# Expert layer: token numbers by one-hot products, rows gathered per tile, part of its weights and statistics made in the layer ahead

## The chip, the cores and the metric

The kernel runs on one core of one Trainium2 chip. The metric is the device time of one launch in microseconds, the median of three runs. A second number, the profiled execution, is one launch under the hardware profiler; all durations below are from it.

## What is computed

`x` is 4096 tokens by 256 numbers (128 sequences of 32 tokens). Six layers are added to it in turn, each on a layer norm of `x`. The three that the change touches:

```python
# first layer (x0): softmax attention of 32 queries over 257 keys, 16 heads of 16
scores = jnp.einsum('bhqd,bhkd->bhqk', q, k) / np.sqrt(D_K)
scores = jnp.where(mask[:, None, :, :] > 0, NEG, scores)
p = jax.nn.softmax(scores, axis=-1)
x = jnp.einsum('bhqk,bhkd->bhqd', p, v)
...
# fifth layer (a1): softmax self-attention over 32 tokens, 16 heads of 16
attn = jnp.einsum('bhid,bhjd->bhij', q, k) * scale + phi_bias(L)[None, None]
out = jnp.einsum('bhij,bhjd->bhid', jax.nn.softmax(attn, axis=-1), v)
...
# sixth layer (e1): each token goes to one of 8 experts (256 -> 1024 -> 256)
route_prob = jax.nn.softmax(t @ switch_w + switch_b, axis=-1)
routes = jnp.argmax(route_prob, axis=-1)
for e in range(n_experts):
    h = jax.nn.gelu(t @ w1[e] + b1[e])
    out = jnp.where((routes == e)[:, None], h @ w2[e] + b2[e], out)
out = out * jnp.max(route_prob, axis=-1)[:, None]
```

## The kernel before

`x` stays in SBUF as `all_xres`, 128 partitions by 32 tiles of 256. Products that need float32 accuracy are three float16 products of a high and a low part: ScalarE (ACT) rounds to the high part (`hi_...`), VectorE (DVE) or GpSimd (POOL) subtracts it from the source for the low part (`lo_...`). Each layer is one block in which the five engines run their own instruction streams and wait for one another by counting semaphores; the order on an engine is that of the code, written out by hand as one loop body with its stages taken from different steps. Layers are separated: the next block begins when all engines have left the one before.

**x0, softmax_attention.** A loop over 128 sequences. For each, TensorE (PE) makes keys and values, scores in two row groups of 64 rows (`scores`), eight transposes of the probabilities by the identity (`transposes`, L556, each 128 by 128 in float32), and products with the values in column groups of 32 (`attend`). PSUM tile `psT` of 1024 columns holds the transposes; ACT copies it in two pieces (`hi_pT`, L670) and DVE makes the low part in two (`lo_pT`, L804). PE's order in one sequence is keys, transposes, (an x tile's transposes), values, attend, scores.

**a1, self_attention.** 32 steps, each for one x tile (four sequences). The DVE order in a step: `add_max` of the next step (L2485, L2490), `lo_pT` (L2502), the residual of the step before (L2527, "all_xres"), `lo_xn` or `lo_k` of a later pair (L2463), `sum_recip` (L2495, L2497), in some steps `ln` (L176), `extract` (L2511, three times), `lo_ob` (L2518), `lo_q` or `lo_v` of a later pair. POOL spreads queries over heads (`a_qbdh`, `a_qbdl`, L2193), subtracts maxima (L2202), scales by the reciprocal sums (L2208) and adds the bias (L2216).

**e1, sort_tokens ("e1r").** Loads nine constants through SP's queue, makes the statistics of all tiles (`Statistics`, L149, then L152 to L164), and runs over the 32 tiles: normalise on DVE (L176), transpose on PE (L2660), copy on ACT (L2693), logits on PE (L2667). Between tiles, pieces of the expert weights (16 of 128x2048, loaded into two `stage` tiles) are split by ACT (`hi_w`, L2687) and DVE (`lo_w`, L2741): half of them here, half in the later part. Then the routing: softmax, the first best expert as a one-hot (`oh`), counts over tiles by two products with `tri` and `ones` (`psR`), two scans, and for every token its place in a list of 39 slots of 128 rows, each slot holding tokens of one expert. Every place of the list in HBM (`e_rows`, 5 MB) is filled with a pad row first (L2823), and POOL then scatters 32 tiles of rows (x, probability, token number, mean, reciprocal deviation) into it by indirect DMA (L2831), from row buffers that ACT fills with x (L2708) and DVE with the other numbers (L2809, L2811).

**e1, expert_tiles ("e1t").** 39 slots. SP loads a slot's rows from `e_rows` (L2890). DVE normalises (L3043), PE transposes (L2905) and makes the hidden products in two halves (`psH`, L2921 and L2922), ACT takes the low half sums out (`take_low`, L2971), DVE adds the bias (`add_bias`, L3059, four per half), ACT makes gelu (L2979) and its high part (`hi_hid`, L2987), POOL the low part (`lo_hid`, L3015), PE the second products (`psY`, L2933), DVE the result (L3067 to L3074), and POOL scatters it to the output (L3023).

## Time and profile before

| | before |
|---|---|
| median of 3 runs | 2874.72 us (2873.59 to 2875.07) |
| profiled execution, its own time | 2873.39 us |
| its span, first to last instruction | 2871.6 us |
| mean granted TensorE clock over the span | 0.933 of full |
| PE busy | 2442.8 us, 85% |
| VectorE (DVE) busy | 2156.5 us, 75% |
| ScalarE (ACT) busy | 1948.5 us, 68% |
| GpSimd (POOL) busy | 1579.3 us, 55% |

The busy time of an engine is the sum of its instructions; PE's ends are modelled and overlap, so 85% is an average over stages that are limited by different things. In the profile's picture of the span in 40 slices, x0 lies in the first third, a1 from about 2160 us on, e1r from 2444 us, e1t from 2586 us to the end. The TensorE clock is given as a share of 2.4 GHz: 1.00 is that, 0.50 is 1.2 GHz.

### The profile page before, as it was taken

What the parts mean: (1) busy time and instruction counts of PE and PEld (TensorE: products, weight loads), DVE (VectorE), ACT (ScalarE), POOL (GpSimd) and SP (SyncE); (2) the same over time, 40 slices, a digit from 0 to 9 for tenths busy, and PEclk for the clock granted to TensorE, in tenths of its full rate; (3) what the DMA queues carried; (4) which work ended last, traced back from release to release, by engine and by line L of the source; (5) the groups of instructions that cost most, each with busy time, mean ns of one, the idle gap of its engine ahead of it and who ended that gap; (6) DMA issues with size and microseconds to landing.
All of it is one profiled execution on the core that took longest, in us unless ns stands there. A gap on an engine that the chain in (4) does not pass through costs nothing. (4 is left out here: it accounts for less than half of the span.)

```text
span 2871.6 us, 96041 instructions
## 1 busy us (share of the span) xinstructions
PE 2442.8 (85%) x37734; PEld 1929.7 (67%) x37734; DVE 2156.5 (75%) x4991; ACT 1948.5 (68%) x4323; POOL 1579.3 (55%) x1680
## 2 busy tenths in 40 slices
PE   3999999999946999994969999999957887508997
PEld 2788888888834777762548888888846666506665
DVE  4899999999965999984447677777757887645665
ACT  2788888888847999962437777777736665335554
POOL 3777777777723555531027666766626776053444
PEclk9999999999976999997979999999978999559999
DMA  5222222222100000000022122212100000641110
GB/s 156 63 73 73 71 70 70 70 70 70 48 16 1 1 1 1 1 1 31 1 70 69 55 66 69 69 54 68 52 18 2 2 2 2 222 162 42 42 39 27
DMA packets 120676, 145.06 MB, mean 51 GB/s; under 512 B 12912, under 2 KB 111632, under 8 KB 118064
## 3 DMA queue, kind: packets, MB, share of 16 engines
q1 hardware_dynamic: 115568, 124.40, 14.5%
q0 software_dynamic: 4672, 14.57, 1.4%
q8 instruction: 308, 5.05, 0.7%
q14 instruction: 128, 1.05, 0.1%
HBM read 123.71 MB, written 15.22 MB: 48 GB/s over the span
## 5 line engine op out<-in xcount | busy, mean ns | idle before, releaser
L2068 DVE TENSOR_TENSOR_SCAN m_s<-m_a,m_psBx 128x2048 f32<-128x2048 f32 x64 | 282.7, 4417 | 21.6 <-PE m_psBx L1843 18.8
L1364 DVE SCALAR_TENSOR_TENSOR x_pTl<-x_psS,x_pTh 128x1024 f16<-128x1024 f32 x128 | 156.7, 1225 | 173.8 <-ACT x_pTh L1272 173.8
L662 ACT ACTIVATE x_prob<-x_prob,x_low 128x257 f32<-128x257 f32 x512 | 253.5, 503 | 9.8 <-DVE x_low L789 9.6
L1854 PE MATMUL m_psS<-m_s,all_ident 128*128 128x256 f32 x1024 | 238.4, 386 | 0.9 <-DVE m_s L2068 0.9
L1854 PEld LDWEIGHTS m_psS<-m_s,all_ident 128*128 128x128 f32 x1024 | 190.7, 191 | 43.3 <-issue 18.2
L789 DVE CUSTOM_DVE_ANT_0 x_prob<-x_psS,x_masked,x_prob 128x256 f32<-128x256 f32 x512 | 216.0, 477 | 1.1 <-PE x_psS L546 0.9
L1975 ACT ACTIVATE m_a<-m_dt,m_rate 128x248 f32<-128x248 f32 x512 | 205.8, 489 | 5.0 <-DVE m_s L2068 4.6
L678 ACT ACTIVATE x_kh<-x_psK,x_bk 128x256 f16<-128x256 f32 x256 | 107.5, 470 | 118.1 <-PE x_psK L430 118.1
L3015 POOL TENSOR_TENSOR e1t_hidl<-e1t_g,e1t_hidh 128x512 f16<-128x512 f32 x78 | 92.8, 1189 | 144.3 <-ACT e1t_hidh L2987 144.3
L804 DVE SCALAR_TENSOR_TENSOR x_pTl<-x_psT,x_pTh 128x512 f16<-128x512 f32 x256 | 163.2, 677 | 0.9 <-PE x_psO L572 0.9
L1053 POOL TENSOR_TENSOR x_qbdh<-x_qh,all_mask4h 128x1024 f16<-128x1024 f16 x32 | 60.6, 1895 | 181.1 <-DVE x_ql L1345 181.1
L1045 POOL TENSOR_TENSOR x_ctxl<-x_ctx,x_ctxh 128x512 f16<-128x512 f32 x128 | 149.6, 1168 | 10.7
L1285 ACT ACTIVATE x_vh<-x_psV 128x512 f16<-128x512 f32 x128 | 76.4, 597 | 115.9 <-PE x_psV L1092 115.9
L335 POOL TENSOR_TENSOR x_ctxl<-x_ctx,x_ctxh 128x512 f16<-128x512 f32 x128 | 149.0, 1164 | 10.7
L430 PE MATMUL x_psK<-x_ctxh,x_wkh 128*128 128x256 f16 x512 | 141.6, 277 | 5.7 <-POOL x_ctxl L335 5.0
L1266 ACT ACTIVATE x_psS<-x_psS 128x1024 f32<-128x1024 f32 x128 | 129.0, 1008 | 24.3 <-PE x_psS L1186 24.3
L1092 PE MATMUL x_psK<-x_ctxh,x_wkh 128*128 128x256 f16 x512 | 141.6, 277 | 3.3 <-POOL x_ctxl L1045 3.0
L670 ACT ACTIVATE x_pTh<-x_psT 128x512 f16<-128x512 f32 x256 | 138.9, 594 | 6.3 <-PE x_psT L556 2.1
L3059 DVE SCALAR_TENSOR_TENSOR all_xres<-e1t_psH,e1t_bias,all_xres 128x128 f32<-128x128 f32 x312 | 87.5, 343 | 72.8 <-ACT all_xres L2971 72.8
L1092 PE MATMUL x_psV<-x_wvh,x_ctxh 128*128 128x256 f16 x512 | 141.0, 275 | 0.6 <-issue 0.6
L1092 PE MATMUL x_psK<-x_ctxh,x_wkl 128*128 128x256 f16 x512 | 140.7, 275 | 0.0
L430 PE MATMUL x_psK<-x_ctxh,x_wkl 128*128 128x256 f16 x512 | 140.7, 275 | 0.0
(554 smaller groups left out, 10247.5 us busy)
## 6 DMA issues: line engine op xcount, KB each, us to landing
x_ctx<-in_ctxT SPq DMA_DIRECT2D x64, 1024.0 KB, 6.2
x_mraw<-in_mask SPq DMA_DIRECT2D x128, 128.5 KB, 2.8
e1r_stage<-in_L_ffn_w SPq DMA_DIRECT2D x16, 1024.0 KB, 5.1
e_rows<-e1r_pad POOLq DMA_DIRECT2D x1, 5070.0 KB, 19.5
e1t_row<-e_rows SPq DMA_DIRECT2D x39, 130.0 KB, 2.1
all_xres<-in_x SPq DMA_DIRECT2D x1, 4096.0 KB, 14.5
x_vxr<-x_vx SPq DMA_DIRECT2D x128, 32.0 KB, 3.6
x_vxr<-x_vx SPq DMA_DIRECT2D x96, 8.0 KB, 2.3
```

Source lines behind the costliest of these rows:

```text
L335: pool.tensor_tensor(lo[:, j], src, hi[:, j], ALU.subtract).then_inc(ctx_split, 1)
L430: last = pe.matmul(out, a, b, start=m == 0, stop=m == len(prods) - 1)
L662: act.activation(prob[c % 4][:, h, :], prob[c % 4][:, h, :], ACT.Exp, bias=low[c % 4][:, h:h + 1], scale=-1.0, accum_out=sm[c % 2][:, h:h ...
L670: act.activation(pT[c % 2][0][:, kt, :], psT[:, kt * 512:(kt + 1) * 512], ACT.Copy, scale=PS)\
L789: dve.tensor_tensor_reduce(prob[c % 4][:, h, 0:LAST], psS[:, to:to + LAST], masked[gp][:, j, 0:LAST], -SC, prob[c % 4][:, h, LAST:S2], ALU ...
L804: dve.scalar_tensor_tensor(pT[c % 2][1][:, kt, :], psT[:, kt * 512:(kt + 1) * 512], PS, pT[c % 2][0][:, kt, :], ALU.mult, ALU.subtract).th ...
L1045: pool.tensor_tensor(lo[:, j], src, hi[:, j], ALU.subtract).then_inc(ctx_split, 1)
L1092: last = pe.matmul(out, a, b, start=m == 0, stop=m == len(prods) - 1)
L1364: dve.scalar_tensor_tensor(pT[c % 4][1][:].rearrange("p r k n -> p (r k n)"), psS[c % 2][:], PS, pT[c % 4][0][:].rearrange("p r k n -> p ( ...
L1854: last = pe.matmul(psS[:, h * ST:(h + 1) * ST], con["ident"][:], S[h][:, :, m, :], start=m == 0, stop=m == NS - 1)
L1975: last = act.activation(A[h][:, :, m, 1:T], dt[c % 2][:, h, :].rearrange("p (b t) -> p b t", t=T)[:, :, 1:T], ACT.Exp, scale=rate[:, h, m: ...
L2068: dve.tensor_tensor_scan(rows(S), rows(A), psBx[:], 0.0, ALU.mult, ALU.add).then_inc(scan_done, 1)
```

## The change

Four parts.

1. **x0.** A transpose of 128 rows becomes two of 64 rows (one for each row group), with a 64x64 piece of the identity as the moving operand: 16 matmuls for 8. The results of a row group lie in one bank, and `hi_pT` and `lo_pT` take a bank each time (the same 2 x 128x512).
2. **a1.** Each of the 32 steps also splits a quarter of an expert weight piece (ACT `hi_w` and DVE `lo_w`, 128x512) and makes the `bn_stats` of the x tile finished in the step before (`count`). SP loads ten constants and eight 1 MB pieces, and writes each finished x tile to HBM (`x_dram`). Some of a1's tiles (`qp`, `K`, `vp`, `V`, `qbd`, `pT`) now lie in the part of the weight tile `ea_w` that is filled later; a1 and e1 share one scope ("ea").
3. **sort_tokens.** No statistics loop and no constant loads. Normalising alternates between DVE and POOL with four buffers. Four pieces of the weights are split in the tile loop, the last four after it: ACT scales the stage tile in place and rounds it (`scale_w`, two 128x2048 each), POOL subtracts (128x2048). The token list is made by matmuls: one-hot of the place in a tile (`oh_in`, 128 per token tile) times one-hot of the slot, with the tile number and with the row number as value (`named`), summed over 32 tiles in `psI` (128x78); from it the token number of each place (`token`). The pad fill, the row buffers and the 32 scatters are gone; only 4 numbers a token are written to `x_dram`.
4. **expert_tiles.** The rows of a slot are gathered from `x_dram` by indirect DMA on POOL's queue, three slots ahead, instead of loaded by SP. ACT's and DVE's orders within a slot are new.

```diff
 (x0, TensorE)
                 for kt in range(2):
                     for h in range(4):
-                        last = pe.transpose(psT[:, kt * 512 + h * P:kt * 512 + (h + 1) * P],
-                                            prob[c % 4][:, h, kt * P:(kt + 1) * P], con["ident"][:])
+                        for r in range(RG):
+                            rows, to = slice(64 * r, 64 * r + 64), r * 512 + (kt * 4 + h) * 64
+                            last = pe.transpose(psT[:, to:to + 64], prob[c % 4][rows, h, kt * P:(kt + 1) * P],
+                                                con["ident"][rows, rows])
...
 (x0, ScalarE; VectorE's lo_pT likewise)
-                for kt in range(2):
-                    act.activation(pT[c % 2][0][:, kt, :], psT[:, kt * 512:(kt + 1) * 512], ACT.Copy, scale=PS)\
-                        .then_inc(pt_hi, 1)
+                for r in range(RG):
+                    act.activation(turned(pT[c % 2][0], r), strip_of(psT, r), ACT.Copy, scale=PS).then_inc(pt_hi, 1)
...
 (a1, SyncE)
+            for g in range(NT):
+                if g % 4 == 0:
+                    wait(sync, w_lo, g)
+                    sync.dma_start(stage[:], d["L1_ffn_w"][g // 4]).then_inc(w_in, 16)
+                if g:
+                    keep_rows(sync, g - 1)
...
 (a1, ScalarE and VectorE)
+            def hi_w(i, c):
+                g = i * 2 * U + c
+                act.wait_ge(w_in, (g // 4 + 1) * 16)
+                act.activation(ahead.W[:, g // 4, 0, quarter(g)], stage[:, quarter(g)], ACT.Copy, scale=WS).then_inc(w_hi, 1)
...
+            def lo_w(i, c):
+                g = i * 2 * U + c
+                dve.wait_ge(w_hi, g + 1)
+                dve.scalar_tensor_tensor(ahead.W[:, g // 4, 1, quarter(g)], stage[:, quarter(g)], WS,
+                                         ahead.W[:, g // 4, 0, quarter(g)], ALU.mult, ALU.subtract).then_inc(w_lo, 1)
+
+            def count(i, c):
+                g = i * 2 * U + (c - 1)
+                dve.wait_ge(x_done, g + 1)
+                dve.bn_stats(ahead.stats[:, g * 6:(g + 1) * 6], xres[:, g * D:(g + 1) * D]).then_inc(ahead.counted, 1)
...
 (sort_tokens, ScalarE behind its tile loop)
+            act.wait_ge(meta_ready, 4)
+            act.dma_start(x_dram[0:TOK, D:ROW].rearrange("(t p) k -> p t k", p=P), meta[:]).then_inc(meta_out, 16)
+            scale_w(LATE - BY_POOL)
+            act.wait_ge(tile_ready, 1)
+            act.activation(named[:, :, 1, :], oh_tile, ACT.Copy, scale=row[:]).then_inc(row_ready, 1)
+            for k in range(LATE - BY_POOL + 1, LATE):
+                scale_w(k)
...
 (sort_tokens, GpSimd)
+            for k in range(LATE - BY_POOL, LATE):
+                hi, lo = halves(k)
+                pool.wait_ge(w_hi, k + 1)
+                pool.tensor_tensor(lo, stage[k % 2][:], hi, ALU.subtract).then_inc(w_lo_pool, 1)
...
 (sort_tokens, VectorE)
+            did(dve.tensor_tensor(oh_tile, slot[:].unsqueeze(1).to_broadcast([P, NT, SLOTS]),
+                                  at_hi[:].unsqueeze(2).to_broadcast([P, NT, SLOTS]), ALU.is_equal))
+            did(dve.tensor_tensor(named[:, :, 0, :], oh_tile, tile[:].unsqueeze(2).to_broadcast([P, NT, SLOTS]), ALU.mult))
+            dve.sem_inc(tile_ready, 1)
...
-                pool.indirect_dma_start(rows_dram, bass.IndirectOffsetOnAxis(ap=idx[c][:], axis=0), row[c][:],
-                                        None).then_inc(placed[c], 16)
...
 (expert_tiles, ScalarE)
                     if exists(i, c, 0):
-                        take_low(i, c, 0)
                         if exists(i, c, 1):
                             hi_xn(*at(i, c, 1))
+                        take_low(i, c, 0)
+                        take_low(i, c, 1)
                         gelu(i, c, 0)
                         hi_hid(i, c, 0)
-                        take_low(i, c, 1)
                         gelu(i, c, 1)
...
 (expert_tiles, GpSimd)
+            def gather(i, c):
+                s = i * U + c
+                wait(pool, o_done, s - U + 1)
+                pool.indirect_dma_start(row[c][:], None, x_dram, bass.IndirectOffsetOnAxis(ap=token[:, s:s + 1], axis=0))\
+                    .then_inc(row_in[c], 16)
...
 (expert_tiles, VectorE)
-                    if exists(i, c, 2):
-                        normalise(*at(i, c, 2))
                     if exists(i, c, 1):
                         lo_xn(*at(i, c, 1))
                     if exists(i, c, 0):
                         add_bias(i, c, 0)
                         add_bias(i, c, 1)
+                    if exists(i, c, 2):
+                        normalise(*at(i, c, 2))
```

On VectorE in the self-attention, from `lo_ob` of one step to `lo_pT` of the next, before:

```order
L2518 SCALAR_TENSOR_TENSOR a_obl<-a_o,a_obh 128x256
L2463 TENSOR_TENSOR a_ql<-a_psQK,a_qh 128x512
L2485 SCALAR_TENSOR_TENSOR a_prob<-a_psS,all_phi 128x256 x2
L2490 TENSOR_REDUCE a_mx<-a_prob 128x16
L2502 SCALAR_TENSOR_TENSOR a_pTl<-a_psT,a_pTh 128x512
```

and with the change (`ea_w` is the weight tile, and also the name of the tiles that a1 has lent from it):

```order
L2566 SCALAR_TENSOR_TENSOR a_obl<-a_o,a_obh 128x256
L2511 TENSOR_TENSOR ea_w<-a_psQK,ea_w 128x512
L2578 BN_STATS ea_stats<-all_xres 128x6
L2572 SCALAR_TENSOR_TENSOR ea_w<-a_stage,ea_w 128x512
L2533 SCALAR_TENSOR_TENSOR a_prob<-a_psS,all_phi 128x256 x2
L2538 TENSOR_REDUCE a_mx<-a_prob 128x16
L2550 SCALAR_TENSOR_TENSOR ea_w<-a_psT,ea_w 128x512
```

Two instructions are put in ahead of the next step's `add_max`.

On ScalarE in the sort phase, from the last tile of the loop to the end of the block, before:

```order
L2693 ACTIVATE e1r_row<-e1r_psX 128x256 x4
L2702 ACTIVATE e1r_ex<-e1r_lg 128x256
L2687 ACTIVATE e_w<-e1r_stage 128x2048
L2708 ACTIVATE e1r_row<-all_xres 128x256 x4
L2687 ACTIVATE e_w<-e1r_stage 128x2048
L2708 ACTIVATE e1r_row<-all_xres 128x256
L2708 ACTIVATE e1r_xn<-all_xres 128x256 x2
L2708 ACTIVATE e1r_pad<-all_xres 128x256
```

and with the change:

```order
L2772 ACTIVATE e1r_xnT<-e1r_psX 128x256 x2
L2776 ACTIVATE e1r_ex<-e1r_lg 128x256
L2778 DMA e_x<-e1r_meta 128x32x4
L2764 ACTIVATE e1r_stage<-e1r_stage 128x2048
L2767 ACTIVATE ea_w<-e1r_stage 128x2048
L2781 ACTIVATE all_xres<-all_xres,ea_row 128x32x39
L2764 ACTIVATE e1r_stage<-e1r_stage 128x2048
L2767 ACTIVATE ea_w<-e1r_stage 128x2048
L2764 ACTIVATE e1r_stage<-e1r_stage 128x2048
L2767 ACTIVATE ea_w<-e1r_stage 128x2048
L2764 ACTIVATE e1r_stage<-e1r_stage 128x2048
L2767 ACTIVATE ea_w<-e1r_stage 128x2048
L2671 UNCONDITIONAL_BRANCH
```

The copies of x into row buffers (L2708) are gone; the second `scale_w` stands behind the activation that waits for VectorE's one-hot of the slots (L2781).

On ScalarE in one slot of the expert tiles, before:

```order
L2965 ACTIVATE e1t_bias<-e_b 128x8
L2971 ACTIVATE all_xres<-e1t_psH 128x512
L2958 ACTIVATE e1t_xnp<-e1t_psX 128x256
L2979 ACTIVATE e1t_g<-all_xres 128x512
L2987 ACTIVATE e1t_hidh<-e1t_g 128x512
L2971 ACTIVATE all_xres<-e1t_psH 128x512
L2979 ACTIVATE e1t_g<-all_xres 128x512
L2987 ACTIVATE e1t_hidh<-e1t_g 128x512
```

and with the change:

```order
L3010 ACTIVATE e1t_bias<-ea_b 128x8
L3003 ACTIVATE e1t_xnp<-e1t_psX 128x256
L3016 ACTIVATE all_xres<-e1t_psH 128x512 x2
L3024 ACTIVATE e1t_g<-all_xres 128x512
L3032 ACTIVATE e1t_hidh<-e1t_g 128x512
L3024 ACTIVATE e1t_g<-all_xres 128x512
L3032 ACTIVATE e1t_hidh<-e1t_g 128x512
```

Both copies of the low sums (L2971, now L3016) stand together ahead of the first gelu, and the high part of the next slot's x ahead of them.

## Rows read from the trace of the kernel before

**Rows 1.** Windows: busy (count) of PE, PEld, DVE, ACT, POOL; clock, DMA share, GB/s.

```profile
100.00:760.00 660.00, 648.77 (x12743) 545.62 (x12741) 634.38 (x1993) 554.43 (x1711) 471.28 (x700) 1.00 0.25 71
2160.00:2420.00 260.00, 209.84 (x3686) 174.24 (x3686) 216.68 (x412) 169.04 (x301) 192.56 (x147) 0.97 0.01 2
2470.00:2513.00 43.00, 40.26 (x191) 37.10 (x191) 30.23 (x43) 23.54 (x39) 0.00 (x0) 0.50 0.56 190
2620.00:2850.00 230.00, 212.57 (x1684) 151.37 (x1684) 140.91 (x437) 134.61 (x271) 113.97 (x102) 1.00 0.13 38
```

**Rows 2.** Timeline of PE and its loads in one sequence of x0: start, us, count.

```profile
302.66 0.27 PE L430 MATMUL x_psV<-x_wvh,x_ctxl 128*128 128x256 f16 x1
302.86 0.21 PE L572 MATMUL x_psO<-x_pTh,x_vh 128*32 128x64 f16 x4
...
305.43 1.04 PE L556 MATMUL x_psT<-all_ident,x_prob 128*128 128x128 f32 x8
306.31 0.38 PE L450 MATMUL x_psM<-all_ident,x_xn 128*128 128x128 f32 x2
```

**Rows 3.** Timeline of PE at the end of the sort's tile loop.

```profile
2511.83 1.71 PE L2667 MATMUL e1r_psL<-e1r_sw,e1r_row 128*128 128x8 f32 x8
```

**Rows 4.** Timeline of a1, VectorE and GpSimd, at the end of a step.

```profile
2317.07 0.74 DVE L2485 SCALAR_TENSOR_TENSOR a_prob<-a_psS,all_phi 128x256 f32<-128x256 f32 x2
2317.23 1.90 POOL L2193 TENSOR_TENSOR a_qbdh<-a_qh,all_mask4h 128x1024 f16<-128x1024 f16 x1 [2.58 <-DVE a_ql L2463]
```

**Rows 5.** Line L2518 of VectorE: duration ns min/median/max over its 32 instructions.

```profile
L2518 DVE SCALAR_TENSOR_TENSOR a_obl<-a_o,a_obh x32: 425/426/1103, 2178.1 to 2441.8; 128x256 f16<-128x256 f32 x32
```

**Rows 6.** Timeline, three engines, from a1's last residual to the end of the routing.

```profile
2443.83 0.42 DVE L2527 SCALAR_TENSOR_TENSOR all_xres<-a_psY,all_xres 128x256 f32<-128x256 f32 x1 [1.55 <-PE a_psY L2248]
2452.67 0.28 DVE L2720 MEMSET e1r_pad<- 128x260 f32 x1 [8.42 <-DMA e1r_tokid<-in_rt_tokid]
2453.76 10.55 DVE L149 BATCH_NORM_STATS2 e1r_ln_stats<-all_xres  x32
2470.32 0.73 DVE L176 TENSOR_SCALAR e1r_xn<-all_xres,all_mean,all_rstd 128x256 f32<-128x256 f32 x2
2472.33 2.28 DVE L2741 SCALAR_TENSOR_TENSOR e_w<-e1r_stage,e_w 128x2048 f16<-128x2048 f32 x1
2513.58 0.42 DVE L2762 TENSOR_TENSOR e1r_lg<-e1r_psL,e1r_s_bias 128x256 f32<-128x256 f32 x1 [1.81 <-PE e1r_psL L2667]
2515.28 1.89 ACT L2687 ACTIVATE e_w<-e1r_stage 128x2048 f16<-128x2048 f32 x1
2521.94 0.69 DVE L2780 TENSOR_TENSOR_SCAN e1r_inc<-e1r_go_on,e1r_tot 128x256 f32<-128x256 f32 x1
2526.10 0.42 DVE L2795 TENSOR_REDUCE e1r_m<-e1r_lg 128x32 f32<-128x256 f32 x1
```

**Rows 7.** Timeline from the last scatter to the first expert product.

```profile
2579.45 0.96 POOL L2831 DMA_INDIRECT e_rows<-e1r_pad,e1r_idx  x1 [0.30 <-issue]
2585.52 3.65 SPq L2890 DMA_DIRECT2D e1t_row<-e_rows  x8
2587.66 0.87 DVE L3043 TENSOR_SCALAR e1t_xn<-e1t_row 128x256 f32<-128x256 f32 x2 [14.41 <-DMA e1t_row<-e_rows]
```

**Rows 8.** Lines of GpSimd, whole kernel, and the page's DMA issues.

```profile
L122 POOL TENSOR_TENSOR f_w1l<-f0w_stage,f_w1h 128x2048 f16<-128x2048 f32 x1 | 4.1, 4061 | 9.5 <-ACTq L97 9.5
...
e1r_stage<-in_L_ffn_w SPq DMA_DIRECT2D x16, 1024.0 KB, 5.1
```

**Rows 9.** Waits from 2620 to 2850 us: us in total, times, longest.

```profile
ACT e1t_g L2979 <- DVE all_xres L3059: 91.9, 67, 1.8
...
PEld e1t_psY L2933 <- issue: 21.7, 34, 0.8
PE e1t_psY L2933 <- POOL e1t_hidl L3015: 17.2, 34, 0.6
```

**Rows 10.** Timeline of VectorE, expert tiles: the bias additions of one half.

```profile
2689.92 1.12 DVE L3059 SCALAR_TENSOR_TENSOR all_xres<-e1t_psH,e1t_bias,all_xres 128x128 f32<-128x128 f32 x4
```

More of the change, by code:

```diff
@@ L2583, in sort_tokens @@
-def sort_tokens(nc, d, xres, con, norm, W, b1, b2, owner, rows_dram):
-    E, SLOTS, PIECE = 8, owner.shape[1], 2048
-    ID, ROW = D + 1, D + 4
-    NPIECE = 2 * E
-    U, ROUNDS = 8, NPIECE // 4
+        b2 = sp.sb("b2", [P, E * D], F32)
+        owner, token = sp.sb("owner", [P, SLOTS], I32), sp.sb("token", [P, SLOTS], U32)
+        sort_tokens(nc, d, xres, con, norm, ahead, b2, owner, token)
+        expert_tiles(nc, xres, con, ahead, b2, owner, token, out)
+def sort_tokens(nc, d, xres, con, norm, ahead, b2, owner, token):
+    E, SLOTS, ROW = 8, owner.shape[1], D + 4
+    LATE, BY_POOL = 16 - AHEAD, 4
+    W, x_dram, consts = ahead.W, ahead.x_dram, ahead.consts
+    sw, s_bias, tri, ones, desc, slot, place_in, tile, row = (consts[k] for k in (
+        "sw", "s_bias", "tri", "ones", "desc", "slot", "place_in", "tile", "row"))
@@ L2743, in body, with lo_w @@
-            def body(i):
-                for c in range(U):
-                    ln(i, c)
-                    if c % 4 == 3:
-                        lo_w(i, c // 4)
-            run(dve, body)
+            dve.wait_ge(ahead.counted, NT)
+            statistics.finish(dve, norm)
+            dve.sem_inc(stats_ready, 1)
+            def lo_w(k):
+                hi, lo = halves(k)
+                dve.wait_ge(w_hi, k + 1)
+                dve.scalar_tensor_tensor(lo, stage[k % 2][:], WS, hi, ALU.mult, ALU.subtract).then_inc(w_lo, 1)
```

375 lines of the change are left out of this document (192 added, 183 removed).

## The prediction

> **What bounds the kernel now.** I read the windows first, stage by stage [rows 1]. In x0 (100 to 760 us) PE is busy 648.8 of 660 us and VectorE 634.4: both are nearly full, so either can become the bound. The clock is 1.00. In a1 (2160 to 2420) no engine is: PE 209.8, VectorE 216.7 and GpSimd 192.6 of 260 us, a cycle of waits. A step takes 8.6 us. In the sort's tile loop (2470 to 2513) PE is busy 40.3 of 43 us at a clock of 0.50, so PE sets the pace at 1.2 GHz. In the expert tiles (2620 to 2850) PE is busy 212.6 of 230 us; 34 slots in 230 us make 6.76 us each. The waits there tell what the rest is: PE waits for the low part of the hidden values 17.2 us in 34 slots, its weight loads stand 21.7 us ahead of the same products, and ScalarE waits 91.9 us for VectorE's bias additions [rows 9]. That is ScalarE and VectorE taking turns inside a slot, half by half, each half costing VectorE 1.12 us [rows 10].
>
> The timeline around the sort shows the largest stretch without PE work. From a1's last residual at 2443.8 to the first normalised row of the expert tiles at 2587.7 it is 143.8 us [rows 6, 7], and in it nothing overlaps with the layers on either side.
>
> **x0, transposes in halves.** Eight transposes take 0.88 us from the first to what follows, 0.11 each [rows 2]. What limits them? The logit products of the sort have a moving operand of 8 columns and still take 0.214 us each at half clock (1.71 us for 8) [rows 3], so loading 128 float32 columns costs 0.107 us at full clock, which is the same 0.11. The change has 16 loads of 128 columns. If the two row groups load side by side, as it has to be for them to be worth it, they take 0.88 again; if one behind the other, 16 x 0.107 = 1.71, 0.85 more for each of 128 sequences. No row shows float32 loads of two row groups. I take side by side. What is certain is that PE now changes the shape of its array around the transposes. From the last product of the values (0.11 apart within the run) to the first of the column groups is 0.20 us [rows 2], 0.09 more than inside a run. Two more such changes in a sequence are 0.18 us, 23 us in 128 if all of it shows. PE idles 1.7% and VectorE 4% of the time [rows 1], so part is absorbed: I take **+14 us**, between 0 and 23 if loads go side by side, and up to +110 (128 x 0.85) if not. The copies of ScalarE and VectorE keep their count and size.
>
> The Trainium skill (TensorEngine Tiling (Array Packing), Key Properties) says that changing the tiling mode drains TensorE, and the 0.09 us agree. The same page (Theoretical Speedup) gives up to 2x for operands of at most 64 rows; estimated by it, the eight pairs would take half, 56 us less of PE in x0. The row of the 8-column products speaks against that, because there the load has the time and not the moving side.
>
> **a1, two more VectorE instructions a step.** In the cycle, `add_max` of the next step follows `lo_q` without a pause [rows 4], and everything behind it (`lo_pT`, PE's attend, `extract`) waits for it. So what is put ahead of it adds in full. `count`: 10.55 us for 32 bn_stats is 0.33 [rows 6]. `lo_w` at 128x512: a quarter of 2.28 is 0.57 [rows 6], I take 0.60. Together 32 x 0.93 = 29.8 us. Then the neighbour: `a_obl` (two inputs in SBUF) takes 0.43 us as a rule but up to 1.10 [rows 5], when GpSimd works at the same time. `lo_w` also has two inputs in SBUF, and in the step that ends with `lo_q` GpSimd begins its spread of 1.90 us 0.16 us after `add_max` would begin [rows 4]; `lo_w` begins 0.33 after that point and would stand until GpSimd is done, some 1.55 us. This meets 14 of the even steps; of it 0.47 comes back, since the next spread then no longer meets `a_obl`. 14 x (1.55 - 0.47) = 15. Sum **+44 us**, from +30 (no block) to +52 (blocked also by other spreads). ScalarE's 0.6 us a step for `hi_w` lies in its 35% of idle time [rows 1], and the DMAs (8 MB loaded, 4 MB written over 275 us, at a DMA share of 0.01 now) cost nothing.
>
> The Trainium skill (SBUF — State Buffer, Who interferes with whom) states this as an exclusive lock of a port pair between GpSimd and a VectorE instruction with two SBUF inputs, held for a whole instruction. By it the block is full and not a slowdown, which is the 1.10 against 0.43 in the row; a share of bandwidth would have made it a few tenths.
>
> **Sort, until the end of its tile loop.** Now 2443.83 to 2513.58, 69.8 us [rows 6]. Away: the wait for the constants behind a1 (to 2452.67, of it 0.75 for the change of block stays), 7.7; filling pad and go_on, 1.1; bn_stats 10.55; four of eight `hi_w` in the loop, each of which puts ScalarE's copies off. The loop takes 43.26 us for 32 tiles, and 32 x 1.17 (PE's eight products at half clock) is 37.4; the rest, 5.9 us over eight pieces, is 0.55 a piece after the first ones' start, so 2.2 back. New: one `count` 0.33, and `lo_w` of the last piece near the end, 1. Sum **-20 us**, the loop ending 49.5 us after the last residual. I keep the clock at 0.50, because PE is busy 94% of the window at that clock and does not leave it [rows 1].
>
> **Sort, behind the loop.** Let R be the end of the loop. Before, the first row of the expert tiles is normalised at R + 74.1 (2513.6 to 2587.7) [rows 6, 7]: routing 14.7, 32 scatters and their landing, then a change of block and a load of 2.1. With the change there are two chains. VectorE's: the scan stands at R + 8.4 now, and GpSimd's first late piece (a 128x2048 subtraction is 4.06 [rows 8], started when ScalarE's two passes of 1.89 [rows 6] are over, R + 8.1) holds it till R + 12.2, 3.8 later; the places are then known at R + 16.8, the slot one-hot and its product with the tile number (1248 columns each, about 1.4) at R + 20.5. The weights': ScalarE stands at that one-hot and begins piece 5 at R + 21.8; two passes 3.8, GpSimd 4.1 until R + 29.7; only then is the stage tile free for piece 7, whose load is 5.1 [rows 8], R + 34.9; two passes, 38.7; GpSimd 4.1, R + 42.8. The token numbers (32 products of 78 columns, five short VectorE steps) are there near R + 31, so the weights end it. Change of block 2.6 (the 5.1 us from the last scatter to the first load [rows 7], less its landing), gather 1.0 to issue and 2.4 to land: R + 49. **-25 us**. Both parts of the sort: **-45**, from -36 to -53.
>
> **Expert tiles.** The low sums of both halves are taken together, so VectorE adds the bias of the second half while ScalarE is at the first gelu. ScalarE's 134.6 us / 34 = 3.96 a slot plus one wait of 1.12 - 0.58 makes 4.5 us, VectorE's 140.9 / 34 = 4.1 [rows 1, 10]: both below PE. PE's wait of 17.2 / 34 = 0.51 goes, at most the 0.64 of its loads [rows 9]. The larger, times 38 slots, is **-25 us**; -10 if GpSimd's two more instructions a slot (a gather of about 1 us, as the scatter) hold its low parts back.
>
> **Sum.** +14 +44 -45 -25 = -12 us against the profiled execution's 2873.39, 2861; the median of the runs shown is 1.3 above that execution, so **2862 us**.
>
> **Rivals.**
> 1. *As summed*, within the bounds of its terms (2845 to 2880). Chance 0.50. Three quarters of it is more than 0.2% below 2874.7 (5.7 us, what a measurement of this kernel can tell from none).
> 2. *The halved transposes really run in half the time.* Then VectorE at 96% is what is left, worth 20 us at most in x0; with +14 gone the sum is about 2833. For it: score products of two row groups already run side by side. Against: the 8-column row. 0.10.
> 3. *Loads of the row groups go one behind the other.* +110 in place of +14: 2958, slower. For it: nothing shows a pair of float32 loads. 0.08.
> 4. *Slower through a1 alone*: `lo_w` meets a GpSimd instruction in every step, not in 14. GpSimd is busy 74% of the time there [rows 1]. Then 32 x (0.93 + 1.55) = 79, in place of 44: 2897. It decides from +62 on. Against: in odd steps the place behind `lo_v` has no spread beside it. 0.14.
> 5. *The clock rises* in the sort's loop, because PE now idles 7 us and not 27 ahead of it. The loop is then paced by ScalarE and the pieces, some 17 us shorter: 2845. 0.10.
> 6. *The expert order does nothing*: the slots keep 6.76 us, another alternation takes the place. 2887, slower. 0.08.
>
> Faster: 0.37 of case 1, with 0.10 and 0.10 of cases 2 and 5, 0.57. Slower: 0.08, 0.14 and 0.08 of cases 3, 4 and 6, and 0.01 of case 1, 0.31. Same: the rest of case 1, 0.12. The range from 2838 to 2898 holds cases 1, 4, 5 and 6 and leaves out 2 and 3, 0.18.
>
> **What would show it.** In x0: 5.5 to 5.7 us a sequence, transposes 0.9 us in total with an 0.2 us gap on both sides; if 1.7, rival 3. In a1: a two-step of 19.9 us in place of 17.2, with a `lo_w` of about 2.1 us in every second step and 0.6 in the others. In the sort: a tile loop at 0.50 that takes 41 us, ScalarE waiting for the one-hot of the slots, and a last GpSimd subtraction ending the block near R + 43. In the expert tiles: a slot of 6.13 us without a PE wait for `e1t_hidl`. Wrong by most would be the x0 term, which is multiplied by 128 and has no row of its own.

## The result, and the profile after

| | before | changed |
|---|---|---|
| median | 2874.89 us (2873.59 to 2875.56, 4 runs) | 2898.78 us (2897.48 to 2901.02, 4 runs) |
| span of the profiled execution | 2871.6 us | 2899.2 us |
| ratio | | 1.0081, 95% interval 1.0068 to 1.0094 |

The change makes the kernel 24 us slower, where 12 us faster was forecast; 2898.78 lies just above the end of the forecast range, 2898. Read at the same landmarks in both traces, the 27.6 us between the spans come from these stages:

| stage, from and to | before | changed | difference | forecast |
|---|---|---|---|---|
| x0: until the last transpose of probabilities starts | 812.3 | 802.8 | -9.5 | +14 |
| from there until a1's first maximum | 1352.0 | 1352.6 | +0.6 | 0 |
| a1: first maximum to last residual | 279.5 | 338.2 | +58.7 | +44 |
| sort: last residual to the end of its tile loop | 69.8 | 53.5 | -16.3 | -20 |
| sort: end of the loop to the first normalised slot | 74.1 | 47.6 | -26.5 | -25 |
| expert tiles: first normalised slot to last result | 276.2 | 293.2 | +17.0 | -25 |
| last result to the end | 7.7 | 11.3 | +3.6 | 0 |

Windows of the changed kernel (PE, PEld, DVE, ACT, POOL busy, clock, DMA share), which answer to [rows 1]:

```profile
100.00:750.00 650.00, 632.32 (x13621) 503.95 (x13620) 633.62 (x1989) 539.89 (x1709) 470.62 (x702) 1.00 0.25 72
2190.00:2420.00 230.00, 172.96 (x2704) 146.38 (x2702) 190.74 (x347) 129.42 (x236) 142.89 (x109) 0.90 0.12 42
2502.00:2545.00 43.00, 37.95 (x185) 35.66 (x184) 12.68 (x19) 18.41 (x36) 25.40 (x16) 0.50 0.29 100
2640.00:2870.00 230.00, 227.45 (x1565) 149.79 (x1563) 141.40 (x408) 128.63 (x253) 135.36 (x125) 1.00 0.12 37
```

In the expert tiles PE is now busy 227.5 of 230 us, almost without a wait, and yet does fewer products than before (x1565 for x1684 in the same 230 us). In a1 the clock has fallen from 1.00 in that stretch to 0.90.

**x0.** Timeline of PE; it answers to [rows 2]:

```profile
309.06 0.27 PE L442 MATMUL x_psK<-x_ctxh,x_wkl 128*128 128x256 f16 x1
309.26 0.71 PE L570 MATMUL x_psT<-all_ident,x_prob 64*128 64x64 f32 x16
309.90 0.31 PE L482 MATMUL x_psM<-all_ident,x_px 128*96 128x128 f32 x1
```

The 16 transposes take 0.64 us to what follows, where 8 took 0.88. The start times of the single records show how: the two transposes of a pair, one in each row group, start 0.003 us apart, and from the second pair on one pair follows the other after 0.061 us, where whole transposes followed after 0.109. The 0.64 us also hold a first pair of 0.11 us and 0.15 us from the last pair to the product behind, with its other shape. With the shape change ahead (0.20 after the last key product, 0.11 inside a run) about 0.15 us less a sequence are left; 0.07 of it arrives (9.5 / 128). That VectorE, now busy 633.6 of 650 us, takes up the rest is likely and not shown by a run.

**a1.** The line of `lo_w` (duration ns min/median/max), and the timeline of VectorE and GpSimd at the end of an even step; they answer to [rows 5] and [rows 4]:

```profile
L2572 DVE SCALAR_TENSOR_TENSOR ea_w<-a_stage,ea_w x32: 666/676/2271, 2171.0 to 2492.3; 128x512 f16<-128x512 f32 x32
```

```profile
2444.33 0.42 DVE L2578 BATCH_NORM_STATS2 ea_stats<-all_xres 128x6 f32<-128x256 f32 x1
2444.50 1.89 POOL L2235 TENSOR_TENSOR ea_w<-ea_w,all_mask4h 128x1024 f16<-128x1024 f16 x1 [2.08 <-DVE ea_w L2511]
2444.67 2.27 DVE L2572 SCALAR_TENSOR_TENSOR ea_w<-a_stage,ea_w 128x512 f16<-128x512 f32 x1
2446.86 0.74 DVE L2533 SCALAR_TENSOR_TENSOR a_prob<-a_psS,all_phi 128x256 f32<-128x256 f32 x2
```

The block is where it was foreseen: 13 of the 32 `lo_w` take 2.27 us (14 were forecast), the one shown until 0.55 us after the end of GpSimd's spread at 2446.39; the others take 0.67. A block as whole as this is what the Trainium skill (SBUF — State Buffer, Who interferes with whom) says of two SBUF inputs beside GpSimd.

**Expert tiles.** Waits from 2640 to 2870 us, the longest; they answer to [rows 9]:

```profile
ACT all_xres L3016 <- PE e1t_psH L2967: 98.5, 62, 1.8
...
DVE e1t_yb L3123 <- PE e1t_psY L2979: 26.8, 32, 1.0
```

Both engines now wait for PE, and PE for nobody. Its timeline shows hidden products (those of the first expert matrix, 32 a slot) 0.125 us apart through the whole slot:

```profile
2708.05 0.28 PE L2966 MATMUL e1t_psH<-e1t_xnp,ea_w 128*128 128x256 f16 x1 [0.20 <-issue]
2708.18 0.23 PE L2967 MATMUL e1t_psH<-e1t_xnp,ea_w 128*128 128x128 f16 x1
2708.30 0.28 PE L2966 MATMUL e1t_psH<-e1t_xnp,ea_w 128*128 128x256 f16 x1
```

Each of these products has a weight address that depends on the slot's expert, and so a register instruction ahead of it. In the profile these stand in the queue behind PE (`PEldq`, its sequencer), with the loads of the expert's number and the waits, ahead of the products that they belong to. The register instructions of the two lines follow each other after 0.124 us, 16 of each in the next slot:

```profile
L2967 PEldq FUSED_REGOPS  x16: 46/46/46, 2708.1 to 2712.0; - x16
```

That is the pace of the products. The sequencer has no lead over the array, and where it loses its lead is seen just ahead of these products. Instructions of one slot, lines L2978, L3099 and L2941 between 2704.5 and 2708.5 us (start of the first and of the last):

```profile
L2978 PEldq FUSED_REGOPS  x8: 46/46/60, 2704.7 to 2705.6; - x8
```

```profile
L3099 DVE TENSOR_SCALAR e1t_xn<-e1t_row x1: 403/403/403, 2706.6 to 2706.6; 128x256 f32<-128x256 f32 x1
```

```profile
L2941 PEldq TENSOR_LOAD <-e_owner x1: 306/306/306, 2707.0 to 2707.0; - x1
```

The sequencer has issued the register instructions of a slot's second products by 2705.6. Next in the program are two transposes, which wait for the normalised rows; VectorE makes these at 2706.6, behind its bias additions. Only at 2707.0 can the sequencer load the next expert's number. In the kernel before it was there 0.2 us after the last of them:

```profile
L2933 PEldq FUSED_REGOPS  x8: 46/46/60, 2696.8 to 2697.7; - x8
```

```profile
L2883 PEldq TENSOR_LOAD <-e_owner x1: 300/300/300, 2697.9 to 2697.9; - x1
```

There it has a lead over the array, and the first 18 hidden products of the slot that starts at 2692.97 us take 1.49 us, 0.083 apart and not 0.125. Over all 1248 hidden products, the distance from one to the next is under 0.1 us for a quarter of them before and for 2% in the changed kernel. So the theory is: the late normalise makes PE's sequencer stand 1.2 us a slot, and it has no spare time to make that up.

### The profile page after: what moved, and what is told of

It is laid out like the page before. It is cut to its first block and busy times, and to the rows that moved or that the text cites. A ratio compares the mean times of both kernels' runs of the same rounds, so it can differ in the third digit from the quotient of the medians.

```text
span 2899.2 us, 97754 instructions
## 1 busy us (share of the span) xinstructions
PE 2486.8 (86%) x38790; PEld 1920.0 (66%) x38790; DVE 2180.6 (75%) x4939; ACT 1935.3 (67%) x4320; POOL 1614.3 (56%) x1709
## 5 line engine op out<-in xcount | busy, mean ns | idle before, releaser
L2966 PE MATMUL e1t_psH<-e1t_xnp,ea_w 128*128 128x256 f16 x624 | 159.8, 284 | 2.3 <-issue 0.5
L2290 PE MATMUL a_psO<-ea_w 128*64 128x128 f16 x1536 | 98.5, 264 | 71.8 <-DVE ea_w L2550 71.8
L2235 POOL TENSOR_TENSOR ea_w<-ea_w,all_mask4h 128x1024 f16<-128x1024 f16 x64 | 121.3, 1899 | 61.5 <-DVE ea_w L2511 61.5
L2290 PEld LDWEIGHTS a_psO<-ea_w 128*64 128x64 f16 x1536 | 92.6, 138 | 80.8 <-DVE ea_w L2550 80.8
```

Source lines behind the costliest of these rows:

```text
L2290: last = pe.matmul(out, a, b, start=m == 0, stop=m == len(prods) - 1)
L2966: pe.matmul(at, wh, x[:, :, cc, :], start=cc == 0, stop=False)
```

## The experiments

**The order in the expert tiles.** Rival: the gathers on GpSimd's queue. Four kernels take the orders apart. On the changed kernel, VectorE's normalise first:

```diff
+                    if exists(i, c, 2):
+                        normalise(*at(i, c, 2))
                     if exists(i, c, 1):
                         lo_xn(*at(i, c, 1))
                     if exists(i, c, 0):
                         add_bias(i, c, 0)
                         add_bias(i, c, 1)
-                    if exists(i, c, 2):
-                        normalise(*at(i, c, 2))
```

> The changed kernel with one edit: in the expert tiles VectorE's normalise stands first in a slot again, as before the change. Theory A: PE's sequencer stands about 1.25 us a slot at the wait for the normalised rows, which lies ahead of its register instructions; with the wait gone the slot is 6.2 us and not 7.2, the whole about 38 us shorter than the changed kernel (near 2861). Rival B: the slot is long because GpSimd's gathers (about 1 us each, and VectorE's last addition 0.77 us and not 0.48 beside them) hold the low parts and the result; then the order of normalise gives under 5 us (2894 or more). Rival C: PE's sequencer is bound by its own register instructions alone; then the slot stays at 7.2 us wherever normalise stands.

Measured: 2860.38 us, ratio to before 0.9949 (0.9933 to 0.9964). The expert tiles take 253.4 us and not 293.2, a slot 6.22 and not 7.23 (from one result to the next, mean of 38). The load of the expert's number follows the last register instruction at once again (lines L2978 and L2941):

```profile
L2978 PEldq FUSED_REGOPS  x8: 46/46/60, 2697.1 to 2698.1; - x8
```

```profile
L2941 PEldq TENSOR_LOAD <-e_owner x1: 302/302/302, 2698.4 to 2698.4; - x1
```

The reverse edit, on the kernel before (normalise behind `add_bias`):

> The kernel before with one edit: VectorE's normalise of the expert tiles stands behind the bias additions, as in the changed kernel. If the wait of PE's sequencer for the normalised rows is what costs (theory A), the slot of 6.77 us grows here too, though ScalarE's order is the old one: by 0.3 to 1 us, 12 to 38 us in all. If the old alternation of ScalarE and VectorE hides it (rival), within 4 us of before.

Measured: 2952.05 us, 1.0274 (1.0256 to 1.0292). The effect is there and twice the upper end that was expected: the expert tiles take 355.6 us and not 276.2, a slot 8.79 and not 6.77. The sequencer stands 2.84 us a slot here (table below), more than in the changed kernel. That this is because ScalarE's old order puts VectorE's second bias additions, and the normalise behind them, late in the slot fits the order and was not tested by itself.

ScalarE's new order alone, on the kernel before (`hi_xn`, `take_low` twice, then the gelus; SP's loads kept):

```diff
-                        take_low(i, c, 0)
                         if exists(i, c, 1):
                             hi_xn(*at(i, c, 1))
+                        take_low(i, c, 0)
+                        take_low(i, c, 1)
                         gelu(i, c, 0)
                         hi_hid(i, c, 0)
-                        take_low(i, c, 1)
                         gelu(i, c, 1)
```

> The kernel before with ScalarE's new order in the expert tiles alone (rows still loaded by SP, VectorE's normalise first as before). Theory: this order is where the 23 us come from that the expert tiles gain once normalise stands first; the time from the first normalised row to the last result falls from 276 to 253 to 258 us. Rival: the gain comes from the gather or the waits that are plain now and not from the order; then it stays above 270.

Measured: 2851.11 us, 0.9919 (0.9904 to 0.9934); the expert tiles take 253.5 us. And the gather with both old orders (the first diff, and this one reversed):

> The changed kernel with both old orders in the expert tiles (VectorE's normalise first, ScalarE's low sums half by half), so that only the gather by GpSimd is new there. Theory: the expert tiles take what they took before, 276 us, up to 282 with GpSimd's second indirect transfer beside VectorE's last addition. Rival: the gather alone costs or gives more than 8 us.

Measured: 2882.97 us, 1.0026 (1.0017 to 1.0036); the expert tiles take 274.6 us. So the gather costs nothing there, ScalarE's order gives 22.7 us (276.2 to 253.5), and VectorE's takes 39.8 (253.4 to 293.2).

The wait that the theory names can be measured in each of these traces: the time from the end of the last register instruction of a slot's second products to the load of the next expert's number, median of 36 or 37 slots.

| kernel | normalise | ScalarE's order | sequencer, us a slot | expert tiles |
|---|---|---|---|---|
| before | first | old | 0.20 | 276.2 |
| before, normalise late | late | old | 2.84 | 355.6 |
| before, ScalarE's new order | first | new | 0.20 | 253.5 |
| changed | late | new | 1.31 | 293.2 |
| changed, normalise first | first | new | 0.20 | 253.4 |
| changed, both old orders | first | old | 0.20 | 274.6 |

It is 0.20 wherever normalise stands first. In the changed kernel it is 1.11 us a slot longer, 43 us in 39 slots, for a stage that is 39.8 us longer. In the kernel before with a late normalise it is 2.64 us longer, 103 us in 39 slots, of which 79.4 arrive; with ScalarE's old order PE has waits of its own in a slot [rows 9], which may take in the rest.

**The transposes in halves**, alone on the kernel before (part 1 of the change):

```diff
-                        last = pe.transpose(psT[:, kt * 512 + h * P:kt * 512 + (h + 1) * P],
-                                            prob[c % 4][:, h, kt * P:(kt + 1) * P], con["ident"][:])
+                        for r in range(RG):
+                            rows, to = slice(64 * r, 64 * r + 64), r * 512 + (kt * 4 + h) * 64
+                            last = pe.transpose(psT[:, to:to + 64], prob[c % 4][rows, h, kt * P:(kt + 1) * P],
+                                                con["ident"][rows, rows])
```

> The kernel before with the 64-row transposes of the first layer alone. Theory (from the trace of the changed kernel, where the layer ends 9.5 us earlier): the two row groups work at the same time, the transposes take 0.6 us and not 0.88 in a sequence, and the total is 9 us shorter (2866). Rival: the 9.5 us come from something else in the changed kernel's layout (other addresses in SBUF); then within 3 us of before. The prediction on record has +14.

Measured: 2867.6 us, 0.9969 (0.9958 to 0.9979), 7.8 us less than the kernel before in the same series; the last transpose starts at 801.6 us, as in the changed kernel (802.8) and not as before (812.3). So these us belong to the transposes.

**The self-attention.** First `lo_w` and `count` ahead of `lo_q` and `lo_v` in every step:

```diff
                     lo_ob(i, c)
+                    lo_w(i, c)
+                    if exists(i, c, -1):
+                        count(i, c)
                     if fe:
                         (lo_q, lo_v)[c % 2](*front)
-                    if exists(i, c, -1):
-                        count(i, c)
-                    lo_w(i, c)
```

> The changed kernel with one edit in the self-attention: VectorE's lo_w and count stand ahead of lo_q / lo_v and not behind them, so that lo_w runs before GpSimd's spread starts. Theory: in 13 steps lo_w takes 2.27 us and not 0.67, which is GpSimd's spread of 1.90 us; all 32 are then 0.6 to 0.7 us, and 13 x 1.6 = 21 us are saved less about 6 for a_obl or another instruction beside GpSimd, and perhaps up to 10 more if the clock no longer falls to 0.89: between -12 and -30 against the changed kernel. Rival: the spread is only put off by the later lo_q and blocks the next two-input instruction, or the front of the next step comes later by the same; then within 5 us of the changed kernel.

Measured: 2903.33 us, 1.0093 (1.0078 to 1.0109), a1 at 340.4 us: the theory fell in this form. `lo_w` in even steps is free (0.69) and in most odd ones 1.21, since the second spread now runs beside it, `a_obl` is back at 1.10 there, and in 13 steps between 2200 and 2440 us `lo_w` waits for `hi_w`, 7.3 us in all. Of the 20.9 us that the blocks had cost, 6.4 are left at `lo_w` and 5.7 have gone to `a_obl`; with the 7.3 of the wait this is nearly all of them. So the place has to differ by step, and `hi_w` to come earlier:

```diff
 (VectorE)
                     lo_ob(i, c)
+                    if c % 2 == 0:
+                        lo_w(i, c)
+                        if exists(i, c, -1):
+                            count(i, c)
                     if fe:
                         (lo_q, lo_v)[c % 2](*front)
-                    if exists(i, c, -1):
-                        count(i, c)
-                    lo_w(i, c)
+                    if c % 2 == 1:
+                        count(i, c)
+                        lo_w(i, c)
 (ScalarE)
+                    hi_w(i, c)
                     extract(i, c)
...
-                    hi_w(i, c)
```

> The changed kernel, edit in the self-attention alone: lo_w and count stand ahead of lo_q in even steps and behind lo_v in odd steps, and ScalarE's hi_w stands ahead of extract. The run with lo_w ahead of both showed it free (0.69) in even steps, blocked (1.21) in odd ones, and waiting 0.58 for hi_w. Theory: both are now free, lo_w 0.67 to 0.69 in all 32, a_obl still 1.1 in odd steps, no wait for hi_w; two steps take 19.1 us at a clock of 1.00 and a1 is 15 to 28 us shorter than the changed kernel's 338.2 us between the first maximum and the last residual. Rival: the low part is not what the step waits for, and a1 stays above 332.

Measured: 2887.26 us, 1.0047 (1.003 to 1.0064); a1 takes 318.1 us, 20.1 less. Its line of `lo_w`:

```profile
L2572 DVE SCALAR_TENSOR_TENSOR ea_w<-a_stage,ea_w x32: 666/680/685, 2166.2 to 2468.4; 128x512 f16<-128x512 f32 x32
```

No `lo_w` is held any more. The 13 blocks were 13 x 1.60 = 20.8 us. That this is nearly the 20.1 us gained is in part chance: `a_obl` is held again (7.2 us more than in the changed kernel; the prediction had 14 x 0.47 = 6.6 for it), the wait for `hi_w` is gone, and the clock is 0.93 and not 0.90.

The expert tiles take 300.9 us in this run and 293.2 in the changed kernel, with the same code. That goes with the series and not with the edit: four kernels were measured together (this one, the two behind it and the one with piece 5 early), on a chip that no other experiment ran on. They have 299.8 to 301.8 us, and the changed kernel and the three others of its code here (with late normalise and ScalarE's new order) have 293.2 to 293.9. In those four PE's sequencer stands 1.47 to 1.58 us a slot and not 1.31, which is 6 to 11 us in 39 slots; why it does is open, and none of the four has normalise first. So from these four kernels only the stage that was edited is compared. The self-attention itself is steady: six traces of the changed one's code, from three chips, take 338.2 to 341.0 us.

Then `lo_w` of the self-attention left out:

```diff
 (SyncE)
-                    wait(sync, w_lo, g)
+                    wait(sync, w_hi, g)
...
 (GpSimd, once)
+            pool.memset(ahead.W[:, 0:AHEAD, 1, :], 0.0)
...
 (VectorE)
-                    lo_w(i, c)
```

> The changed kernel without the 32 lo_w of the self-attention (the low parts of half of the expert weights are zero here, made by one GpSimd memset at the start of the layer); hi_w, count and the transfers stay. Theory: per step count 0.34 is left, two steps take 17.9 us and a1 falls from 338.2 to near 291 (279.5 of before, 11 for count), less if the clock's loss belongs to lo_w as well. Rival: the transfers or hi_w cost too; then a1 stays above 300.

Measured: one run, 2868.84 us; a1 takes 287.7 us. (The total has some 10 us more for the GpSimd memset, which lies ahead of a1's first maximum.) So `lo_w` stands for 50.5 of the 58.7 us, and `count`, `hi_w` and the transfers together for 8.2, under the 11 of `count` alone that were expected. 32 x 0.6 + 20.8 = 40 us are `lo_w`'s own time, blocked part included; 10 more are left (about 13, since `a_obl` is held 3.4 us more in this run). The clock is the candidate: with `lo_w` left out it is 0.99 from 2190 to 2420 us, with it 0.90. To test that, PE gets more work where it waits, and the results are overwritten:

```diff
                 g, turn, t = i * 2 * U + c, c // 2, c % 2
+                wait(pe, o_ext, g)
+                for _ in range(8):
+                    pe.matmul(psO[:, 0:256], Wp[0][:, 0, 0:P], Wp[0][:, 0, :], start=True, stop=True)
                 pe.wait_ge(pt_lo, g + 1)
                 if t == 0:
                     pe.wait_ge(v_ready, i * U + (c // 2 + 1))
-                wait(pe, o_ext, g)
```

> The changed kernel with eight more products (128x256, results overwritten) in each step of the self-attention, placed where PE waits 2.4 us for VectorE's low part of the probabilities; they take 0.86 us. Theory: of the 58.7 us that the layer is longer, about 12 come from the clock, which is at 0.89 in the mean and not 1.00; with PE less idle the clock is back near 1.00 and the layer 6 to 12 us shorter, in spite of more work. Rival: the clock's level costs nothing here, since PE waits anyway; then the layer's time is the same or up to 4 us longer.

Measured: one run, 2890.29 us; a1 takes 322.7 us, 15.5 less than the changed kernel, with 256 products more. The blocks are all still there, 13 `lo_w` of 2.27 us, so the gain is not from them. Its window (columns as above):

```profile
2190.00:2420.00 230.00, 182.53 (x3015) 152.49 (x3012) 198.83 (x363) 134.01 (x247) 149.21 (x115) 0.99 0.13 42
```

The control, the same eight products in the kernel before:

> The control for the filling products: the kernel before, whose clock in the self-attention is 1.00 already, with the same eight products in each step. If they help by the clock alone, they give nothing here: the layer stays at 279.5 us or gets up to 8 longer. If it falls by more than 3 us, they help in another way.

Measured: 2873.45 us, 0.9999 (0.999 to 1.0008); a1 279.3 us for 279.5. Its clock was and stays 1.00:

```profile
2190.00:2420.00 230.00, 213.27 (x3596) 178.70 (x3593) 189.65 (x373) 149.05 (x267) 175.77 (x135) 1.00 0.01 2
```

The products help only where the clock had fallen. Step by step it is the same: a pair of steps (from one maximum to the second next) takes 20.2 to 22.5 us in the middle of the changed kernel's stage, and with the filling products it takes 20.2 ten times of fifteen; 19.9 were forecast, at a clock of 1.00. So the clock is shown as a cost of the changed self-attention, about 10 to 15 us of the 58.7.

**The sort.** Piece 5 of the weights ahead of ScalarE's wait:

```diff
             scale_w(LATE - BY_POOL)
+            scale_w(LATE - BY_POOL + 1)
             act.wait_ge(tile_ready, 1)
             act.activation(named[:, :, 1, :], oh_tile, ACT.Copy, scale=row[:]).then_inc(row_ready, 1)
-            for k in range(LATE - BY_POOL + 1, LATE):
+            for k in range(LATE - BY_POOL + 2, LATE):
                 scale_w(k)
```

> The changed kernel with one edit in the sort: ScalarE makes the late weight piece 5 before it waits for the one-hot of the slots, not behind. Theory: the four late pieces are the chain that ends the block (last GpSimd subtraction until 2590 us); piece 7 is then loaded 9 to 13 us earlier, and VectorE's routing, held 2 us more, ends the block near 2581: the time from the end of the tile loop to the first normalised row falls from 47.6 to 36 to 40 us. Rival: GpSimd's subtractions hold VectorE's routing for as much as the weights gain; then it stays above 45.

Measured: 2904.42 us, 1.0097 (1.008 to 1.0114); from the loop's end to the first slot 43.5 us, not 47.6, between theory and rival (the total is hidden by the expert tiles, 301.0 us here). The weights are ready 6 us earlier (GpSimd's last subtraction ends at 2584.0 us and not 2590.1), and VectorE's routing ends the block instead. The timeline shows what holds it, GpSimd's two subtractions in a row (8.46 us):

```profile
2554.62 8.46 POOL L2800 TENSOR_TENSOR ea_w<-e1r_stage,ea_w 128x2048 f16<-128x2048 f32 x2 [13.92 <-ACT ea_w L2767]
2554.65 4.58 DVE L2854 TENSOR_TENSOR_SCAN e1r_inc<-e1r_go_on,e1r_tot 128x256 f32<-128x256 f32 x1
2559.27 3.84 DVE L2856 TENSOR_SCALAR e1r_cnt<-e1r_inc 128x8 f32<-128x8 f32 x1
2563.14 0.17 DVE L2857 CAST e1r_cnt_i<-e1r_cnt 128x8 int32<-128x8 f32 x1
```

The sort's tile loop, 4 us longer than forecast: first all 32 normalisations on VectorE (GpSimd's loop of `xn` removed, VectorE's over all t):

```diff
-            for t in range(0, NT, 2):
+            for t in range(NT):
                 wait(dve, xnT_mm, t - 3)
...
-                if t % 8 == 6:
+                if t % 8 == 7:
                     lo_w(t // 8)
```

> The changed kernel with all 32 normalisations of the sort on VectorE, none on GpSimd. In the changed kernel GpSimd's normalisation takes 3.35 us and not 1.22 four times, each time beside VectorE's low part of a weight piece, and PE then waits 2.9 us. Theory: these four waits go, the time from the last residual to the end of the tile loop falls from 53.5 to 46 to 50 us. Rival: VectorE's 2.28 us for a low part puts its own next normalisation off by as much; then it stays above 52.

Measured: 2898.54 us, 1.0084 (1.0069 to 1.01); 53.4 us to the loop's end, nothing gained: the rival holds. Then `lo_w` three tiles later in addition:

```diff
-                if t % 8 == 7:
-                    lo_w(t // 8)
+                if t % 8 == 2 and t > 8:
+                    lo_w(t // 8 - 1)
+            lo_w(NT // 8 - 1)
```

> The changed kernel with the sort's normalisations on VectorE and each lo_w of its tile loop three tiles later, so that VectorE normalises ahead and doesn't stand at the wait for ScalarE's high part. Theory: the loop's loss against the forecast (53.5 us from the last residual to its end, 49.5 forecast) is VectorE standing there 5.3 us and then taking 2.29, while PE lacks a tile; with lo_w later the 53.5 fall to 47 to 50. Rival: ScalarE's 1.90 us is what PE waits for; then 52 or more.

Measured: 2894.98 us, 1.0074 (1.0059 to 1.0089); 48.8 us, 4.6 less. In the changed kernel VectorE had stood at the wait for `hi_w` four times, 5.3 us each, instead of normalising ahead.

**Together.** Normalise first, `lo_w` placed by step, filling products, piece 5 early and normalisations on VectorE (which had gained nothing alone), then with the later `lo_w` of the sort, with and without the filling products:

> All edits together that helped: normalise first in the expert tiles, lo_w split around lo_q and lo_v with hi_w ahead of extract, the eight filling products in the self-attention, weight piece 5 ahead of the wait, and all normalisations of the sort on VectorE. By the separate runs: 2899 - 38 (normalise) - 20 (lo_w) - 6 to -10 (clock) - 4 (tail) - 5 (sort loop) = 2822 to 2832, below both kernels. If the self-attention gains overlap, up to 2842.

> The combination of the last call with lo_w of the sort's loop three tiles later: 2829 less what that gives alone, 3 to 6 us: 2823 to 2827.

> The same combination without the eight filling products in the self-attention. Theory: its clock is 0.93 there (as in the run with lo_w split), not 0.98, and it is 2 to 8 us slower than with the filling products. Rival: with lo_w split PE no longer idles enough for it to matter; then it is 0 to 4 us faster without them.

Measured: 2829.28 us, 0.9848 (0.9833 to 0.9862); 2824.57 us, 0.9829 (0.9815 to 0.9842); without the filling products 2834.33 us, 0.9866 (0.9851 to 0.9882). The first lies in its range, though the 5 us that it took for the sort's loop were not there (53.4 us). The best is 49 us below the kernel before and 74 below the changed one. The filling products give 2.7 us in a1 (317.8 to 315.1, clock 0.92 to 0.96) where `lo_w` isn't held. The medians differ by 9.8 and the two profiled executions by 1.4, so how much of the 9.8 is theirs is open.

## Why the prediction was wrong, step by step

1. **Expert tiles, the step that failed.** "The larger, times 38 slots, is -25 us": its sum took ScalarE's new order and the two engines' busy time, and left out that the change also puts VectorE's normalise behind the bias additions. That place was in the diff, but neither the sum nor a rival asked who waits for it. PE's sequencer does, in its own order, ahead of the register instructions of 32 products. The prediction held VectorE harmless because its 4.1 us a slot are below PE's time, and gave the order within the slot no price. With normalise first the stage is 253.4 us, 22.8 under before where 25 was forecast; with it late 293.2. This is 39.8 us, more than the whole miss of 37. Rival 6 (another alternation takes its place) had no gain in this stage; the runs show a loss of 17.0, from a cause that it did not name.
2. **x0.** "I take side by side" was right, and the term was mis-sized all the same. It had 0.88 us for the 16 transposes, from a load of 0.107 us; measured are 0.64 with its neighbour's start, and the pairs are 0.061 us apart. The row of 8-column products, loads of 128 rows, didn't bound loads of 64 rows in two groups. -9.5 us and not +14; the shape change ahead cost 0.09 as forecast. Of the two statements of the Trainium skill (TensorEngine Tiling (Array Packing), Key Properties and Theoretical Speedup), both are seen, and the second decides: 0.061 for 0.109 us is close to its "Up to 2×". Rival 2 had this mechanism, with a chance of 0.10. (Its figure of 2833 is also off by its own terms, 2862 - 14 - 20 = 2828.)
3. **a1.** The mechanism stood as written: full addition behind `lo_q`, a block of 1.6 us in 13 steps. 44 against 58.7; what was missing is the clock, taken as 1.00 without a word. It was 0.90 in a longer step with more idle time of PE, and 0.99 once the filling products took some of that idle time.
4. **Sort.** -43 against -45. Behind the loop -26.5 for -25: the chain of the weights ran as forecast, with the last subtraction ending at 2590. In the loop -16.3 for -20: `lo_w` stood in VectorE's order ahead of the next tiles. The term itself also had a wrong count: "PE's eight products" of a tile are two transposes and four logit products (64 and 128 records for 32 tiles), and PE's busy 40.3 us of the window make 1.26 us a tile, not 1.17, so the loop had less to give back than 5.9 us.
5. **The closing 3.6 us** from the last result to the end are open; no experiment was aimed at them. They are not the orders of the expert tiles: every kernel made from the changed one has 11.3 to 11.6 us there, with both old orders too, and the kernel before and every one made from it 7.7 to 7.9.

The terms together, in the profiled executions (2861 forecast, 2901.0 measured): +42 in the expert tiles, -23.5 in x0, +14.7 in a1 (the clock, mostly), +3.7 in the sort's loop, -1.5 behind it and +4.2 in the two stages that were put at nothing, 39.6 us.

Two numbers came near by luck. With normalise first the kernel takes 2860.38 us and the forecast was 2862, but only because x0's error of -23.5 us happened to be made up by +14.7 in a1 and some 9 in the other stages. And rival 4's 2897 is close to 2898.78, though its mechanism isn't what happened: `lo_w` was held in 13 steps and not in all 32, and a1 stayed below the 79 us that it named. Rival 5 did not come about either, the clock in the sort's loop stayed at 0.50; rival 3 is refuted by the pairs that start together.

## What to carry to other kernels

When an instruction is moved, look for who waits for it in program order on the other side, PE's sequencer above all: a wait there costs even when PE has work queued, as soon as the sequencer itself is the slow part (here 0.124 us a product, against 0.083 where it had a lead). In the self-attention, work put into gaps of a cyclic stage was paid in full because it stood on the cycle, a second time where its neighbour blocked it, and a third time through the clock; so price a step by the order of each engine in it, not by idle shares. When a block is removed by moving, check the next two-input instruction beside the same neighbour: here the first move shifted most of it.

## What the runs showed that was not expected

Transposes of float32 in two 64-row groups took 0.64 us for 16, against 0.88 for 8 of 128 rows, with the two of a pair starting together and 0.061 us from pair to pair.

Short VectorE instructions with one input in SBUF can be held by GpSimd too: a minimum of 39 columns with a constant took 3.77 us and a cast of them 3.98 us, beside subtractions of 4.05 us, in the changed kernel's timeline:

```profile
2572.93 8.08 POOL L2799 TENSOR_TENSOR ea_w<-e1r_stage,ea_w 128x2048 f16<-128x2048 f32 x2 [13.55 <-ACT ea_w L2767]
2573.26 3.77 DVE L2888 TENSOR_SCALAR e1r_own<-e1r_own 128x39 f32<-128x39 f32 x1
2577.07 3.98 DVE L2889 CAST e_owner<-e1r_own 128x39 int32<-128x39 f32 x1
2581.08 0.24 DVE L2892 COPY e1r_held<-e1r_psI 128x78 f32<-128x78 f32 x1
```

256 products of no use made a stage faster (a1 338.2 to 322.7 us, one trace), with the granted clock at 0.99 and not 0.90, and did nothing (279.5 to 279.3) where it was 1.00 already.
